# A graph-attention gather loop: its dependent links set apart in the order of each engine, and one of four weight tiles made by VectorE

## The reference

```python
Wh = x @ W_w + W_b
e = f_dst_part[col] + f_row_part[row] + a_b[0]
e = jnp.where(e > 0, e, ALPHA * e)
m = jax.ops.segment_max(e, row, num_segments=N)
ex = jnp.exp(e - m[row])
denom = jax.ops.segment_sum(ex, row, num_segments=N)
att = ex / denom[row]
h_prime = jax.ops.segment_sum(att[:, None] * Wh[col], row, num_segments=N)
```

## Time and profile before

| what | before |
|---|---|
| median of 3 runs (lowest to highest) | 2633.94 us (2624.93 to 2639.57) |
| the profiled execution's own time, and its span | 2636.18 us, 2634.5 us |
| PE, PEld busy | 2068.0 us (78%), 1614.9 us (61%) |
| DVE, ACT busy | 1835.9 us (70%), 1623.0 us (62%) |
| POOL busy | 1218.4 us (46%) |
| gathers (L1282) | 872.0 us busy, first at 754.2, last at 2007.6 us |
| `total` on PE (L1555), first and last start | 790.3, 2107.5 us |
| first `mark` (L1321) | 768.5 us |

### The profile page before, as it was taken

One profiled execution on the slowest core, in us unless ns is written; L12 is line 12 of the kernel. 1 busy time (PEld: TensorE's weight loads), 2 busy tenths in 40 slices (PEclk: granted clock), 3 DMA queues, 4 the chain that ended last, 5 costly groups with the idle time before them and its releaser, 6 DMA issues. The chain is left out here.

```text
span 2634.5 us, 53974 instructions
## 1 busy us (share of the span) xinstructions
PE 2068.0 (78%) x10267; PEld 1614.9 (61%) x10268; DVE 1835.9 (70%) x6190; ACT 1623.0 (62%) x5201; POOL 1218.4 (46%) x1141
## 2 busy tenths in 40 slices
PE   2888666788838878888888788878888856099997
PEld 1444355677726666666666666666666656088886
DVE  7877689899947777777777777777777664145543
ACT  4566375233218878888788788877888864033332
POOL 0000000011157776676676666766773037735555
PEclk9999977799859989898898889998989866599998
DMA  4100000111124433343333333333331065445554
GB/s 143 41 26 28 18 10 19 48 21 24 24 66 116 112 110 95 106 112 93 92 109 96 102 93 100 102 101 101 108 104 55 2 173 136 107 79 92 96 94 61
DMA packets 125797, 211.81 MB, mean 80 GB/s; under 512 B 35583, under 2 KB 78492, under 8 KB 125476
## 3 DMA queue, kind: packets, MB, share of 16 engines
q0 software_dynamic: 71952, 141.08, 22.7%
q1 hardware_dynamic: 48866, 60.24, 7.6%
q10 hardware_dynamic: 4658, 7.46, 1.0%
HBM read 152.62 MB, written 49.70 MB: 77 GB/s over the span
## 5 line engine op out<-in xcount | busy, mean ns | idle before, releaser
L1282 POOL DMA_INDIRECT area<-wh_table,area x860 | 872.0, 1014 | 395.6 <-issue 248.8
L1555 PE MATMUL bank<-area 128*126 x2008 | 563.0, 428 | 80.5 <-ACT area L1484 68.5
L1555 PEld LDWEIGHTS bank<-area 128*126 128x126 f32 x2008 | 396.4, 208 | 188.7 <-issue 126.6
L1321 DVE TENSOR_SCALAR area<-iota_row,area 128x126 f32<-128x126 f32 x1004 | 353.7, 359 | 0.6 <-issue 0.5
L1484 ACT ACTIVATE area<-area 128x126 f32<-128x126 f32 x1004 | 316.2, 387 | 20.6 <-DVE area L1384 18.3
L1475 ACT ACTIVATE area<-iota_row,area 128x126 f32<-128x126 f32 x1004 | 316.0, 388 | 0.0
L2046 POOL DMA_INDIRECT out_dram<-area x108 | 170.1, 1575 | 158.3 <-DVE area L2105 141.6
L1331 DVE TENSOR_REDUCE area<-bank 125x1 f32<-125x512 f32 x251 | 172.6, 688 | 82.3 <-issue 75.1
L515 POOL IOTA acc_mem<- 50x860 f32 x1 | 0.8, 847 | 457.4 <-DVE area L784 457.4
L1575 PE MATMUL bank<-area 128*128 128x250 f32 x800 | 209.2, 407 | 0.3 <-ACT area L1490 0.3
L1586 PE MATMUL bank<-area 128*125 128x256 f32 x800 | 197.5, 390 | 0.0
(11 more groups left out here) (385 smaller groups left out, 4353.4 us busy)
## 6 DMA issues: line engine op xcount, KB each, us to landing
area<-moe_rows SPq DMA_DIRECT2D x54, 264.0 KB, 2.7
area<-wh_table,area POOLq DMA_INDIRECT x860
area<-area SPq DMA_DIRECT2D x19, 387.0 KB
wh_table<-area SPq DMA_DIRECT2D x50, 126.0 KB
xn<-in_x_dram SPq DMA_DIRECT2D x25, 250.0 KB
x_rows<-area SPq DMA_DIRECT2D x25, 250.0 KB
area<-x_rows ACTq DMA_DIRECT2D x24, 250.0 KB
area<-in_L_ffn_expert_w_dram SPq DMA_DIRECT2D x3, 1536.0 KB, 12.0
```

Of the source, the lines that this page charges most:

```text
L1282: g.indirect_dma_start(out=gath[:, (i + GT) % RS, :], out_offset=None, in_=table, in_offset=bass.IndirectOffsetOnAxis(ap=idx_tab[:, i:i + ...
L1321: ins = V.tensor_scalar(xm[:, b, t, :], iota_row[:, :], rowl[:, j % 5, t:t + 1], fdc[:, b, t:t + 1], ALU.is_equal, ALU.mult)
L1555: last = T.matmul(bank[US][0:RW, 0:WROW], sm[:, b, t, :], gath[:, bass.ds(place + t, 1), :].rearrange("p a w -> p (a w)"), start=(t == 0), ...
```

## The change

- **DVE**: the list is reordered so that links of the two chains stand apart: `load_place` behind `group_peak`, `score_sum` ahead of `row_score`, `shifted` behind it; the addition at the end of `score_sum` becomes a stage of its own, `score_edge`; `row_leaky` is followed by the first `mark`, and so on.
- **ACT**: `divide` becomes `own_high`, `own_mid` and `own_low`, with one `apart` tile behind the first and `spread` behind the second. `apart` makes three tiles, `weigh` three.
- **The fourth weight tile**: ACT's new `edge_exp` takes the exponential of one column of `e3`, 128 x 1; DVE's new `own_weight` makes `sm` of tile 3 as (column == row of the edge) x that exponential. `total` waits for it too. It stands between `keep_max` and `gather_up`.
- `rowl` has ten copies, some waits take other values, and the scratch memory grows by ten columns.

```diff
-        rowl = take(5, GT)
+        rowl = take(10, GT)
+        edge_p = take(2)
...
                 def score_sum(s, j):
                     b = j % 2
                     dve.wait_ge(p_q, at(s, 1, 1))
-                    wait(dve, d_e, at(s))
+                    wait(dve, d_e, at(s, 2, -1))
                     V.tensor_reduce(pair.rearrange("p t k -> p (t k)"), bank[QE][:, 0:6 * GT].rearrange("p (x k) -> p x k", k=3),
                                     AX.X, ALU.add).then_inc(d_es, 1)
+
+                def score_edge(s, j):
+                    b = j % 2
                     dve.wait_ge(d_es, at(s, 3, 1))
                     V.tensor_tensor(e1[:, b, :], dst_terms(j), pair[:, :, 0], ALU.add).then_inc(d_es, 1)
...
                     dve.wait_ge(d_es, at(s, 3, 3))
-                    wait(dve, a_s, at(s, 1, -1))
+                    wait(dve, a_s, at(s, 2, -2))
                     V.tensor_tensor(e3[:, b, :], e2[:, b, :], pair[:, :, 1], ALU.subtract).then_inc(d_e, 1)
+
+                def own_weight(s, j):
+
+                    b = j % 2
+                    dve.wait_ge(a_s, at(s, 2, 1))
+                    wait(dve, p_main, at(s, 1, -1))
+                    V.tensor_scalar(sm[:, b, GT - 1, :], iota_row[:, :], rowl[:, j % 10, GT - 1:GT], edge_p[:, j % 2:j % 2 + 1],
+                                    ALU.is_equal, ALU.mult).then_inc(d_e, 1)
...
-                together(dve, [(2, group_peak), (0, shifted), (4, score_sum), (2, row_score), (0, mark(0)), (4, score_leaky),
-                               (2, row_leaky), (0, mark(1)), (4, score_less_max), (2, new_max), (0, mark(2)),
-                               (2, old_less_new), (0, mark(3)), (2, keep_max), (5, gather_up), (-1, load_place)], feed)
+                together(dve, [(2, group_peak), (-1, load_place), (4, score_sum), (2, row_score), (0, shifted), (4, score_edge),
+                               (2, row_leaky), (0, mark(0)), (4, score_leaky), (2, new_max), (0, mark(1)), (4, score_less_max),
+                               (0, mark(2)), (2, old_less_new), (0, mark(3)), (2, keep_max), (4, own_weight), (5, gather_up)], feed)
...
-                def divide(s, j):
...
+                def own_high(s, j):
+
                     act.wait_ge(d_m, at(s, 6, 4))
                     wait(act, p_q, at(s))
-                    A.copy(high, new[0:R, b:b + 1]).then_inc(a_own, 1)
+                    A.copy(own_part(s, j, 0), new[0:R, j % 2:j % 2 + 1]).then_inc(a_own, 1)
+
+                def own_mid(s, j):
...
+                def own_low(s, j):
+
+                    b = j % 2
                     act.wait_ge(a_own, at(s, 3, 2))
-                    A.activation(low, mid, ACT.Identity, bias=left[0:R, b:b + 1], scale=-1.0).then_inc(a_own, 1)
+                    A.activation(own_part(s, j, 2), own_part(s, j, 1), ACT.Identity, bias=left[0:R, b:b + 1], scale=-1.0).then_inc(a_own, 1)
...
+                def apart(tiles):
+
+                    def stage(s, j):
+                        b = j % 2
+                        act.wait_ge(d_x, at(s, 2, 2))
+                        wait(act, a_s, at(s, 2, -2))
+                        for t in tiles:
+                            last = A.activation(dist[:, b, t, :], iota_row[:, :], ACT.Abs, bias=rowl[:, j % 10, t:t + 1], scale=-1.0)
+                            if t == GT - 2:
+                                last.then_inc(a_dist, 1)
+                    return stage
+
+                def edge_exp(s, j):
+                    act.wait_ge(d_e, at(s, 2, 1))
+                    A.activation(edge_p[:, j % 2:j % 2 + 1], e3[:, j % 2, GT - 1:GT], ACT.Exp).then_inc(a_s, 1)
 
                 def weigh(s, j):
                     b = j % 2
                     act.wait_ge(a_dist, at(s, 1, 1))
-                    act.wait_ge(d_e, at(s, 1, 1))
                     wait(act, p_main, at(s, 1, -1))
-                    for t in range(GT):
+                    for t in range(GT - 1):
                         last = A.activation(sm[:, b, t, :], dist[:, b, t, :], ACT.Exp, bias=e3[:, b, t:t + 1], scale=-1.0e12)
                     last.then_inc(a_s, 1)
...
-                together(act, roots, [(3, divide), (2, spread), (3, apart), (3, rescale), (4, weigh), (-1, own_rows)], feed)
+                together(act, roots, [(3, own_high), (3, apart([0])), (3, own_mid), (2, spread), (3, own_low), (4, edge_exp), (3, apart([1, 2])), (3, rescale),
+                                       (4, weigh), (-1, own_rows)], feed)
...
                 def total(s, j):
                     b = j % 2
                     place = pe.snap(places[j % 4], min_val=0, max_val=RS - 1)
-                    pe.wait_ge(a_s, at(s, 1, 1))
+                    pe.wait_ge(a_s, at(s, 2, 2))
+                    pe.wait_ge(d_e, at(s, 2, 2))
```

More of the change, by code:

```diff
@@ L1320, in stage @@
                         dve.wait_ge(d_x, at(s, 2, 1))
-                        ins = V.tensor_scalar(xm[:, b, t, :], iota_row[:, :], rowl[:, j % 5, t:t + 1], fdc[:, b, t:t + 1],
+                        ins = V.tensor_scalar(xm[:, b, t, :], iota_row[:, :], rowl[:, j % 10, t:t + 1], fdc[:, b, t:t + 1],
                                               ALU.is_equal, ALU.mult)
@@ L1446, in own_rows, with own_part @@
                     wait(act, a_dist, at(s, 1, -4))
-                    A.activation(rowl[:, j % 5, :], row_tab[:, bass.ds(first, GT)], ACT.Identity, bias=iota_blk[:, bass.ds(r, 1)]).then_inc(a_row, 1)
-                def divide(s, j):
-                    b = j % 2
+                    A.activation(rowl[:, j % 10, :], row_tab[:, bass.ds(first, GT)], ACT.Identity, bias=iota_blk[:, bass.ds(r, 1)]).then_inc(a_row, 1)
+                def own_part(s, j, k):
                     r = act.snap(blocks[j % 5], min_val=0, max_val=NT - 1)
-                    high, mid, low = (own_all[:, bass.ds(r, 1), k:k + 1].rearrange("p a k -> p (a k)") for k in (3, 4, 5))
+                    return own_all[:, bass.ds(r, 1), 3 + k:4 + k].rearrange("p a k -> p (a k)")
+                def own_high(s, j):
                     act.wait_ge(d_m, at(s, 6, 4))
                     wait(act, p_q, at(s))
-                    A.copy(high, new[0:R, b:b + 1]).then_inc(a_own, 1)
+                    A.copy(own_part(s, j, 0), new[0:R, j % 2:j % 2 + 1]).then_inc(a_own, 1)
+                def own_mid(s, j):
+                    b = j % 2
                     act.wait_ge(a_own, at(s, 3, 1))
-                    A.activation(mid, high, ACT.Identity, bias=new[0:R, b:b + 1], scale=-1.0)
-                    A.activation(left[0:R, b:b + 1], high, ACT.Identity, bias=new[0:R, b:b + 1], scale=-1.0).then_inc(a_own, 1)
+                    A.activation(own_part(s, j, 1), own_part(s, j, 0), ACT.Identity, bias=new[0:R, b:b + 1], scale=-1.0)
+                    A.activation(left[0:R, b:b + 1], own_part(s, j, 0), ACT.Identity, bias=new[0:R, b:b + 1], scale=-1.0).then_inc(a_own, 1)
+                def own_low(s, j):
+                    b = j % 2
                     act.wait_ge(a_own, at(s, 3, 2))
-                    A.activation(low, mid, ACT.Identity, bias=left[0:R, b:b + 1], scale=-1.0).then_inc(a_own, 1)
+                    A.activation(own_part(s, j, 2), own_part(s, j, 1), ACT.Identity, bias=left[0:R, b:b + 1], scale=-1.0).then_inc(a_own, 1)
                 def rescale(s, j):
@@ L1467, in rescale @@
                     A.activation(alpha[0:R, j % 5:j % 5 + 1], gd[0:R, b:b + 1], ACT.Exp).then_inc(a_alpha, 1)
-                def apart(s, j):
-                    b = j % 2
-                    act.wait_ge(d_x, at(s, 2, 2))
-                    wait(act, a_s, at(s, 1, -1))
-                    for t in range(GT):
-                        last = A.activation(dist[:, b, t, :], iota_row[:, :], ACT.Abs, bias=rowl[:, j % 5, t:t + 1], scale=-1.0)
-                    last.then_inc(a_dist, 1)
+                def apart(tiles):
+                    def stage(s, j):
+                        b = j % 2
+                        act.wait_ge(d_x, at(s, 2, 2))
[8 more added lines that the diff above has]
+                    A.activation(edge_p[:, j % 2:j % 2 + 1], e3[:, j % 2, GT - 1:GT], ACT.Exp).then_inc(a_s, 1)
                 def weigh(s, j):
```

2 lines of the change are left out of this document (1 added, 1 removed).

## The result

| what | before | changed |
|---|---|---|
| median of 4 runs each, on one chip (lowest to highest) | 2635.89 us (2624.93 to 2639.57) | 2504.39 us (2500.62 to 2507.53) |
| the profiled execution's own time, and its span | 2636.18, 2634.5 us | 2507.53, 2505.8 us |

The ratio is 0.9507, with a 95% interval of 0.9475 to 0.9539: 131 us, or 4.9%, faster, where 3.4% was forecast. The median lies 6 us under the range of 2510 to 2600.

What follows compares the result with a forecast made beforehand. ACT alone was taken to set slots 4 to 6, ACT and PE slots 7 to 9, VectorE the others. Chunk gains of 3.85 and 3.6 us made 7.45 a pass, 89 us over 12 passes: 2545 us, range 2510 to 2600.

Steps and rivals of the forecast that it cites:

- G0: Start of `gather_up` on DVE in slot 0, forecast 2.35 us behind that slot's `total` on PE, for 3.26 before.
- B: Chunk whose slot 0 stands in the middle of a loop pass; a chunk inside a pass was to gain 3.85 us.
- Rivals 2, 3 and 4: DVE becomes the bound, 2589 us, 20%; slower, DVE far over PE, 2709, 6%; PE held in hidden slots, 2624, 9%.
- Rival 1: Clock stays up, `total` of slot 2 ends 1.8 us earlier: 0.8 a chunk, 19 us, 2526 us; 20%.
- P0 to D1: From `total` on PE in slot 0 to `group_peak` on DVE in slot 1: gain 1.1 us, 0.85 at the loop's end.
- A: Chunk whose slot 0 stands at the start of a loop pass; one across the loop's end was to gain 3.6 us.
- G0 to D1: From `gather_up` in slot 0 to `group_peak` in slot 1, on DVE: 3.70 us less 0.2 of `load_place`.
- P2 to D3: From `total` on PE in slot 2 to `group_peak` on DVE in slot 3: 7.29 us at half clock, gain 0.
- P4 to P0: From `total` in slot 4 to `total` in slot 0, on PE, with five slots at 4.20: 25.7 us, gain 2.0.
- D1 to P2: From `group_peak` on DVE in slot 1 to `total` on PE in slot 2: 4.25 us for 5.07, gain 0.8.
- D3 to P4: From `group_peak` on DVE in slot 3 to `total` on PE in slot 4: 4.25 us for 4.20, no gain (-0.05).
- The DVE slot: DVE's time for one turn of the ten-slot schedule: 4.02 - 0.20 - 0.20 + 0.34 + 0.15 = 4.1 us.

Runs made afterwards that it cites:

- the two shifts of the target: Clearing of the sums ahead of DVE's loop cut into nine pieces in the kernel before, 2618.67 us, and into 101 in the changed kernel, 2525.04 us.
- before_shifted_q: The kernel before with its clearing of the sums cut into nine pieces, so DVE's loop stands eight instructions further on: 2618.67 us, 0.994 of before.
- order_only_q: The kernel before with the new DVE and ACT lists, all four tiles on ACT, DVE's loop target where the changed kernel's is: 2526.62 us, 0.9588.
- weights_only_q: The kernel before with the fourth weight tile on DVE and the old order on both engines, DVE's loop target moved: 2610.01 us, 0.9904.
- place_last: The changed kernel with `load_place` back at the end of DVE's list: 0.9796 and 0.991 of the kernel before, both on slow chips.

## Why the prediction was wrong in size and mostly right in kind

What came as written: ACT is no longer late and PE is the next limit from slot 5 on; three `apart` and three `weigh` tiles a group; `fetch` of slot 4 waits 0.45 for the low part (0.5); G0 is 2.13 behind P0 in B (2.35, of which no row gave the 0.35); `total` of slot 2 mostly at the lower clock level; POOL's wait for room down by 115 us (90). POOL stayed clear of the path only just: ACT waited 6.9 us for batches, as shown above. Rivals 2, 3 and 4 did not come: DVE's slot is 3.95, not 4.36 or 5.0. Rival 1 came in part: from P2 to G2 a chunk takes 3.77 on average for 3.93, since in a third of the chunks it takes 3.3 to 3.5 and not 4.02.

The sum said 7.45 a pass and the trace says 10.54. The 3.1 between them, term by term:

- **Where the pass of the loop ends, "DVE idles 3.33 on "issue" ahead of the reduction. I leave that as it is, and take 0.85 there."** This step failed most: P0 to D1 of A gained 2.99. The difference between A and B in P0 to D1 was to grow by 0.25 and shrank by 1.45: **+1.7** a pass, or 20 us, and the two shifts of the target put 19 and 20 us on the second stall alone. The second stall of 2.10, behind the reduction, stood in the trace and I didn't read it; and I took the stalls for a property of the branch, when one of them is a property of where the code lies. The Trainium skill ("Runtime: NRT & Kernel Launch", Instruction fetch mechanics) says that a taken branch stalls when its target isn't in the fetch window. The trace agrees in kind for the first stall, which is there in all four kernels of the set. From it I concluded that the stalls stay whatever the order; before_shifted_q shows that the second goes when the target moves by eight instructions.
- **"G0 to D1 3.70 less 0.2 of load_place", and G0 at 2.35.** `load_place` gives 0.43 there, and G0 comes 0.2 sooner: P0 to D1 of B gained 1.54 for 1.1. **+0.9** a pass for both chunks. The 3.70 was also a poor row to start from: it is the longest of the 24 in the trace, whose median is 3.34, and the 6.96 it stands in compares with a mean of 6.60.
- **"P2 to D3, at half clock, 7.29 as now: 0."** It gained 0.43 and 0.47: 0.30 of it is `load_place` again, which stands ahead of D3 too and which I counted in slot 0 alone. The rest is the clock: in 8 of 23 chunks `total` of slot 2 takes 2.97 to 3.27 us at a granted clock of 0.59 to 0.65, where it takes 3.80 at 0.50. **+0.9**.
- **"five slots at 4.20".** PE's own slot is 4.09, so P4 to P0 gained 2.42 and 2.27 for 2.0: **+0.7**. In the earlier trace rows the first weight load of `total` starts with its first matmul, at 1449.88; in the changed kernel it runs ahead, beside `turn`. The weight loads (PEld) of the two, before:

```profile
1449.88 1.60 PEld L1555 LDWEIGHTS bank<-area 128*126 128x126 f32 x8
```

and changed, where the matmul starts at 1425.07:

```profile
1424.96 1.61 PEld L1586 LDWEIGHTS bank<-area 128*126 128x126 f32 x8
```

The same holds in every chunk: in slots 5 to 0 the weight load leads by 0.01 us before, and by 0.11 changed and in order_only_q. I had called 4.20 PE's "own work ... without a gap". Most likely it had 0.11 of waiting for ACT's last tile in it, which no idle time shows; that ACT is the cause is argued from ACT's own 4.20, and no run tests it alone.

- **D1 to P2, "gain 0.8"**: 0.42 and 0.36, **-0.8**. The low part starts 2.08 behind D1 (1.95), and DVE's last operation on the score 2.43 behind it, when the sum had the exponential at 2.37. In 11 of 23 chunks `total` then waits for `gather_up` of slot 1, which is not in the sum. **D3 to P4, "-0.05"**: -0.15 and -0.20, **-0.25**.

**The DVE slot** was taken at 4.1 and is 3.95, close by luck, since its terms were off: 0.20 for the link of `score_edge` where nothing came, 0.20 for `load_place` where 0.29 came, and 0.34 for the operation where 0.16 came. The Trainium skill ("VectorE: DVE Perf Modes", Rules for kernel authors) says to minimize the count of chained operations and not the semaphores; as the prediction reads it, the new order then brings nothing. For the order of the links the trace agrees, with D to G at 3.33 before and 3.39 in order_only_q; what fell was G to D, by the register work of `load_place`. That the operation counts in full is not what the trace shows: 0.16 and 0.25 of 0.34. On the link the forecast was wrong to go by the idle 0.20 in the row.

**The shares.** I had given the order 55 us and it brings 92. By the pieces order_only_q gains 7.5 a pass over before_shifted_q, which is 90 us over 12: P0 to D1 gives 3.0 of it (9.00 to 7.54 in A, 6.63 to 5.07 in B), with the `load_place` of slot 0, P4 to P0 2.8 (27.85 to 26.32, 27.72 to 26.44), and P2 to D3 1.3. The ends of the chunk, which hang on DVE, are the order's almost alone: weights_only_q has 6.73 for P0 to D1 in B.

## What to carry to other kernels

Read every idle time behind a loop's branch, and before a small change in a loop is credited or blamed, run the kernel with a few more instructions ahead of the loop: that alone moved this one by 16 us. Register work is best put behind a long operation of the same engine: the move of `load_place` took 0.29 us out of a DVE slot of 4.02. "No idle time" doesn't show that an engine is at its own pace, if its weights or operands come just in time. A part that relieves an engine may show little alone (9 us for the tile, 18 to 19 on top of the order), so it has to be timed together with its fellow before it is dropped.

## What was not expected of the hardware

- In the loops of these kernels DVE pauses at every 128th instruction of its stream, with 0.30 to 0.47 us for the step in most places, and with 2.2 to 2.3 us (median) when the place comes four instructions behind a taken branch.
- Register work between two DVE operations (`load_place`) costs 0.29 to 0.43 us in the open, and nothing that can be seen behind a reduction of 0.69 (D to G 3.55 changed, 3.63 in place_last).
- An independent operation starts 0.08 to 0.11 behind a one-column operation on ACT; a dependent link of the high, middle and low chain started 0.31 and 0.41 behind.
- The kernel that took 2632 to 2636 us in some sets took 2932 to 2976 in others, with 0.70 us for many register and semaphore instructions of DVE and ACT in stretches. That it belongs to the chip isn't shown: chip number 9 took 2634 us, and eight minutes later 2976. What makes the stretches wasn't found.
